# Second expert products half a round later, images unrolled, and the causal mask by a GpSimd select after the exponentials

## The chip, the cores and the metric

One core of a Trainium2 chip runs the whole program. The metric is device time in microseconds, the median of several executions. A profile records one execution of its own. The core has five engines that matter here: TensorE (PE, its weight loads PEld), VectorE (DVE), ScalarE (ACT), GpSimd (POOL) and SyncE (SP), which issues most DMAs. Each works through its own list of instructions in order, and they meet at semaphores.

## The reference

For 8 images of 1024 tokens with 96 channels: `x = x + moe_conv(groupnorm(x))`, then `t = t + attention(layernorm(t))`, then `t = t + moe_ffn(layernorm(t))`.

```python
# conv block, 8 experts, 2 of them gated in for each token (softmax over the two)
h = gelu(x @ W1[e] + b1[e]);  y = h @ W2[e] + b2[e];  out = sum_e gate[e] * y
# attention, 6 heads of 16 channels, causal over 1024 tokens
att = softmax(where(causal, q @ k.T / 4, -inf));  y = att @ v;  out = y @ w_proj.T + b_proj
# token block, 4 experts (hidden 384 in both blocks), the two largest probabilities, renormalised
```

Every expert is computed for every token; the gates of the others are zero.

## The kernel before

**Split precision.** An activation is kept as the sum of a high and a low half-precision part. A first-layer product of 128 hidden rows and 512 tokens (`first_layer`, out of `w1h`, `w1l` and `xah`, `xal` or `xch`, `xcl`) is three matmuls into one of two banks `ps_u`. ScalarE reads the bank twice with a gelu: to `hid` (32 bits, L933) and to `hidh` (16 bits, L934). GpSimd subtracts, `hidl = hid - hidh` (L628). The second layer (`second_layer`) takes for each tile of 128 tokens six products of 96 columns with `hidh` and then three with `hidl`, into `ps_y`. VectorE multiplies the four tiles of a group by the gates and adds them to `acc`, `x1` or `xo` (`combine`, L1104), and frees the bank.

**Rounds and slots.** A group is one expert on 512 tokens. An iteration has 16 groups of the conv block (phase 0) and 8 of the token block (phase 1), of different images. `rounds` yields for each round the group that goes up (first layer) and the one that goes down (second layer), which is the group before. A round has four slots, with `j` the slot within the round: first-layer product `j` at slots 0, 1 and 2; second-layer tiles none, 0, 1, and 2 with 3 at slots 0 to 3. The wait for all of a group's `hidl` (`hl_ready`) stands in front of the first `hidl` product of tile 0, so behind the first-layer product of slot 1. `hidh` and `hidl` have two buffers.

**Chores.** The rest of the images' work is placed into slots by hand (`schedule`): norms (`ln1`, `ln2`, `gn_...`), routing, the biases (`bias_a`, `bias_c`), `qk` and `val`, and the 72 row maxima of an image (`max`, banks `ps_r`, reduced by VectorE at L1156), one a slot from slot 8. `maxima` then turns them and SyncE writes them as two more rows of `qs`. `ks` and `qs` are loaded through `qk_dram` once the scores of the image before are done.

**Softmax stage.** After the experts come 24 steps of `SOFT_STEPS`, each three heads by 128 keys by up to 512 queries. TensorE's order is scores of step n, then values of step n - 2 (`soft_scores`, `soft_values`). Scores go to five banks in turn (three of `ps_r`, two of `ps_u`). ScalarE takes the exponential into one of three `probs` buffers (L965) and TensorE multiplies with `vaug` into `ps_y`. On the 16 steps at the diagonal a fourth to sixth product per step, `mask_k` by `identb`, adds a very negative number where the key lies after the query.

**Iterations.** `walk` has iterations 0, 1 and 2 written out, 3 to 6 as a loop on every engine (`Fori`; `Count` turns counters into expressions of the loop's register), and 7 to 10 written out. Iteration 0 has the conv block alone and splits the weights, 1 has no token block, 8 is attention alone with its maxima, 9 and 10 have the token block alone.

Of the kernel before, what the change touches and what calls it, by code (L numbers as in the profile page):

```python
# [48 lines left out]
FIRST_LOOP, END_LOOP = 3, NIMG - 1  # L49
# [4 lines left out]
class Count:  # L54


    def __init__(self, per):
        self.per, self.it, self.k = per, None, 0

    def enter(self, it):  # L60
        self.at_entry = self.k
        self.it, self.k = it, self.k - FIRST_LOOP * self.per

    def leave(self):
        n = self.k + FIRST_LOOP * self.per - self.at_entry
        assert n == self.per, (n, self.per)
        self.it, self.k = None, self.at_entry + (END_LOOP - FIRST_LOOP) * self.per

    def value(self, times=1, plus=0):
        k = self.k * times + plus  # L70
        return k if self.it is None else self.it * (self.per * times) + k
# [18 lines left out]
def walk(eng, counts, iteration):  # L90
# [3 lines left out]
    with eng.Fori(FIRST_LOOP, END_LOOP) as it:  # L94
        for c in counts:
            c.enter(it)
        iteration(it, True, True, True)
    for c in counts:
        c.leave()
    iteration(NIMG - 1, True, True, True)  # L100
# [92 lines left out]
def schedule(it):  # L193
# [42 lines left out]
    beside_c = [(1, "bias_c", 0), (4, "bias_c", 1), (5, "ln1", 0), (6, "ln1", 1), (10, "ln1_apply", 0),  # L236
# [36 lines left out]
def shared_uses():  # L273

    return sum(CHORES[name][1] for phase in schedule(None) for at in phase.values() for name, _, _ in at)


# [15 lines left out]
SOFT_STEPS = [(t, c, j) for t in range(2) for c in range(NC) for j in range(TC * (c + 1))]  # L293


def build(nc, x, cWg, cbg, cW1, cb1, cW2, cb2, w_attn, b_attn, w_proj, b_proj,
          fWg, fbg, fW1, fb1, fW2, fb2, out):
    nc.disable_value_cache = True
    with ExitStack() as ctx:
# [24 lines left out]
        mask_k = sb("mask_k", [P, P], BF16)  # L324
# [20 lines left out]
        hidh = sb("hidh", [P, 2, HT, CH], F16)  # L345
        hidl = sb("hidl", [P, 2, HT, CH], F16)
# [94 lines left out]
        s_full, p_ready = sem("s_full"), sem("p_ready")  # L441
        pv_step = sem("pv_step")
# [29 lines left out]
        def _(sp):  # L472
# [91 lines left out]
            walk(sp, [], iteration)  # L564

        @block.gpsimd
        def _(pool):
# [13 lines left out]
            for tile, value in ((identb, 0.0), (mask_q, 0.0), (mask_k, 0.0), (mpart, NEG), (mneg, 0.0)):  # L581
# [17 lines left out]
            g.affine_select(out=mask_k[:], in_=mask_k[:], compare_op=ALU.is_ge, fill=NEG, base=0,  # L599
                            pattern=[[1, P]], channel_multiplier=-1)  # L600
# [42 lines left out]
        def _(pe):  # L643
# [81 lines left out]
            def moes(it, moe_a, moe_c):  # L725
# [5 lines left out]
                for up, down, phase, slots in rounds(moe_a, moe_c):  # L731
# [25 lines left out]
                    if up:  # L757
                        grp.k += 1
# [600 lines left out]
```

## Time and profile before

| | us |
|---|---|
| median of 3 runs | 1535.99 |
| the runs | 1527.34, 1535.99, 1537.08 |
| profiled execution, first to last instruction (its span) | 1533.6 |
| TensorE busy in it | 1324.4 |
| ScalarE busy in it | 934.1 |
| VectorE busy in it | 893.8 |
| GpSimd busy in it | 716.0 |

The span is from an execution that was recorded by the profiler; the runs are executions that were only timed, so what lies around the span is told only by the distance of 1533.6 from those three times. Busy time of an engine doesn't count its waits. A matmul's recorded time has its way through the array in it, so two in a row overlap.

### The profile page before, as it was taken

How to read it: one execution, taken by the hardware profiler on the slowest of the kernel's cores; microseconds unless marked ns; L12 is line 12 of the kernel's file. 1: busy time of each engine (PE TensorE's matmuls, PEld its weight loads, DVE VectorE, ACT ScalarE, POOL GpSimd, SP SyncE). 2: the span in 40 equal slices, each digit the busy share in tenths (PEclk: the TensorE clock that was granted, in tenths of full speed). 3: DMA queues.
4: the chain of work that ended last, by engine and by line, in shares of the span. 5: the costliest groups of instructions: out<-in, count | busy, mean ns of one | idle time of the engine just before them, and what ended most of it. 6: DMA issues, size and time to landing. Idle time of an engine off the chain costs nothing.

```text
span 1533.6 us, 36404 instructions
## 1 busy us (share of the span) xinstructions
PE 1324.4 (86%) x12957; PEld 775.0 (51%) x12957; DVE 893.8 (58%) x2662; ACT 934.1 (61%) x1880; POOL 716.0 (47%) x656
## 2 busy tenths in 40 slices
PE   4778879888898899889898899888998898968978
PEld 1554543565536564466635565365644665333445
DVE  4865593388617784287724886177832866165362
ACT  2566537566675667656675667656676666703755
POOL 4765540467406572367605573075713665000355
PEclk9897998999999999899998999899999999956989
DMA  5000200300021000400004000210003000120100
GB/s 108 12 1 18 46 1 12 75 2 2 12 54 32 2 2 23 71 7 2 2 22 76 1 2 16 52 32 2 2 23 65 1 2 2 38 48 1 23 12 11
DMA packets 37424, 35.14 MB, mean 23 GB/s; under 512 B 26091, under 2 KB 28012, under 8 KB 37234
## 3 DMA queue, kind: packets, MB, share of 16 engines
q1 hardware_dynamic: 20594, 26.37, 8.8%
q10 hardware_dynamic: 16640, 6.29, 1.9%
q8 instruction: 113, 1.85, 0.5%
q14 instruction: 77, 0.63, 0.2%
HBM read 22.62 MB, written 9.63 MB: 21 GB/s over the span
## 4 chain that ended last, share of the span: by engine, by line
PE 30%; issue 26%; POOL 21%; DVE 13%; DMA 4%; ACT 2%; DVEq 1%; POOLq 1%; SPq 1%; ACTq 0%
POOL hidl L628 20%; PE ps_y L647 11%; PE ps_u L647 9%; PE ps_r L647 6%; DVE mpart L1156 4%; PE ps_m L647 3%; DVE xn L1138 1%; DMA ks<-qk_dram 1%; DMA qk_dram<-qk_l 1%; DVE acc L1104 1%; ACT hidh L934 1%; DVE yt L1288 1%; POOLq L608 1%; PE ps_m L666 1%; POOL rstd L609 1%
## 5 line engine op out<-in xcount | busy, mean ns | idle before, releaser
L628 POOL TENSOR_TENSOR hidl<-hid,hidh 128x512 f16<-128x512 f32 x576 | 670.7, 1185 | 686.2 <-ACT hidh L934 684.1
L933 ACT ACTIVATE hid<-ps_u 128x512 f32<-128x512 f32 x576 | 345.0, 599 | 391.8 <-PE ps_u L647 363.2
L1156 DVE TENSOR_REDUCE mpart<-ps_r 128x1 f32<-128x512 f32 (+2 forms) x576 | 297.3, 549 | 94.1 <-PE ps_r L647 79.8
L934 ACT ACTIVATE hidh<-ps_u 128x512 f16<-128x512 f32 x576 | 344.4, 598 | 0.0
L647 PEld LDWEIGHTS ps_y<-w2s,hidh 128*128 128x128 f16 x4608 | 276.4, 101 | 119.2 <-issue 24.1
L647 PE MATMUL ps_y<-w2s,hidh 128*128 128x96 f16 x4608 | 326.3, 210 | 8.0 <-DVE acc L1104 7.2
L647 PE MATMUL ps_r<-ks,qs 96*128 96x512 f16 (+2 forms) x576 | 199.9, 363 | 66.9 <-DVE mpart L1156 39.4
L647 PE MATMUL ps_y<-w2s,hidl 128*128 128x96 f16 x2304 | 231.0, 211 | 26.7 <-POOL hidl L628 26.6
L647 PE MATMUL ps_u<-xah,w1h 97*128 97x512 f16 x408 | 168.7, 414 | 29.8 <-ACT hidh L934 12.8
L965 ACT ACTIVATE probs<-ps_r 128x512 f32<-128x512 f32 (+3 forms) x352 | 152.9, 506 | 57.6 <-PE ps_r L647 57.2
L647 PE MATMUL ps_u<-xah,w1l 97*128 97x512 f16 x408 | 168.1, 412 | 0.0
L647 PE MATMUL ps_u<-xal,w1h 97*128 97x512 f16 x408 | 167.6, 411 | 0.0
L647 PEld LDWEIGHTS ps_y<-w2s,hidl 128*128 128x128 f16 x2304 | 145.0, 101 | 32.6 <-POOL hidl L628 31.7
L647 PE MATMUL ps_y<-probs,vaug 128*32 128x512 f32 (+3 forms) x1152 | 160.0, 499 | 0.1
L965 ACT ACTIVATE probs<-ps_u 128x512 f32<-128x512 f32 (+3 forms) x224 | 104.0, 517 | 27.9 <-PE ps_u L647 27.9
L1104 DVE SCALAR_TENSOR_TENSOR acc<-ps_y,gatesa,acc 128x96 f32<-128x96 f32 x448 | 109.6, 306 | 13.0 <-PE ps_y L647 11.4
L647 PEld LDWEIGHTS ps_r<-ks,qs 96*128 96x128 f16 x576 | 59.8, 104 | 111.0 <-DVE mpart L1156 68.3
L647 PE MATMUL ps_r<-qs,ks 98*128 98x512 f16 (+3 forms) x352 | 99.0, 334 | 9.1 <-DMA qs<-mtl 7.0
L647 PE MATMUL ps_r<-mask_q,identb 128*128 128x128 bf16 x384 | 90.8, 238 | 0.0
L1138 DVE TENSOR_SCALAR xn<-x,mv,rstd 128x96 f32<-128x96 f32 x128 | 83.2, 710 | 8.6 <-POOL rstd L609 8.1
L647 PEld LDWEIGHTS ps_u<-xah,w1h 97*128 97x128 f16 x408 | 42.2, 103 | 68.6 <-ACT hidh L934 27.0
L1047 DVE SCALAR_TENSOR_TENSOR qk_l<-ps_m,qk_h 96x512 f16<-96x512 f32 x32 | 22.0, 687 | 86.6 <-ACT qk_h L988 86.6
(188 smaller groups left out, 1582.0 us busy)
## 6 DMA issues: line engine op xcount, KB each, us to landing
rb<-rsum_dram SPq DMA_DIRECT2D x24, 256.0 KB, 4.2
qs<-qk_dram SPq DMA_DIRECT2D x24, 192.0 KB, 4.9
ks<-qk_dram SPq DMA_DIRECT2D x24, 192.0 KB, 4.8
xin<-in_x_dram ACTq DMA_DIRECT2D x8, 384.0 KB, 4.1
qk_dram<-qk_h SPq DMA_DIRECT2D x16, 192.0 KB, 3.1
qk_dram<-qk_l SPq DMA_DIRECT2D x16, 192.0 KB, 3.5
out_dram<-xo ACTq DMA_DIRECT2D x8, 384.0 KB, 3.0
w_raw<-in_L_conv_W_dram SPq DMA_DIRECT2D x8, 288.0 KB, 5.1
```

Of the source, the lines that this page charges most:

```text
L608: pool.drain()
L609: g.tensor_tensor(dst, dst, power[0:n, 0:dst.shape[1]], ALU.pow).then_inc(done, 1)
L628: g.tensor_tensor(hidl[:, grp.k % 2, j, :], hid[:, j, :], hidh[:, grp.k % 2, j, :], ALU.subtract).then_inc(hl_ready, 1)
L647: return nc.tensor.matmul(dst, lhsT, rhs, start=start, stop=stop, skip_group_check=True)
L666: last = nc.tensor.transpose(ps_m[0:D, P * i:P * (i + 1)], src[:, TC * c + i, :], ident[:])
L933: a.activation(hid[:, j, :], bank[:], ACT.Gelu, scale=1.0 / WS)
L934: a.activation(hidh[:, grp.k % 2, j, :], bank[:], ACT.Gelu, scale=1.0 / WS).then_inc(h_ready, 1)
L965: a.activation(probs[:, n % 3, g, 0:w], soft_bank(k)[:, 0:w], ACT.Exp, scale=float(HD) ** -0.5).then_inc(p_ready, 1)
L1047: return v.scalar_tensor_tensor(out=lo, in0=ps_m[0:D, :], scalar=scale, in1=hi, op0=ALU.mult, op1=ALU.subtract).then_inc(m_free, 1)
L1104: last = v.scalar_tensor_tensor(out=out[:, t, :], in0=ps_y[grp.k % 2][:, D * i:D * (i + 1)], scalar=r.gates[:, t, e:e + 1], in1=acc[:, t, ...
L1138: v.tensor_scalar(dst[:, t, :], src[:, t, :], mv[:, t, 0:1], rstd[:, t:t + 1], ALU.subtract, ALU.mult)
L1156: v.tensor_reduce(mpart[:, h, i, part:part + 1], ps_r[k % 3][:, 0:w], AX, ALU.max).then_inc(mx_free, 1)
```

## The change

It does five things. The loop of `walk` is gone: all iterations are written out. The buffers of `hidh` and `hidl` become three (`HB`), tiles 0 and 1 of the group going down are multiplied at slots 2 and 3, tiles 2 and 3 of it at slots 0 and 1 of the next round; VectorE's additions for a group move to slot 1 of that next round, and `bias_c` 1 from slot 4 to slot 6. In iterations with all three parts the scores of softmax step 0 are issued in the last round of the experts, ahead of the last group's second-layer products. The products with `mask_k` are gone, and so is the tile. In their place GpSimd sets the exponentials behind the diagonal to zero with one select per diagonal step, and the values of those steps wait for it (`causal`).

```diff
-FIRST_LOOP, END_LOOP = 3, NIMG - 1
+FIRST_LOOP = 3
+HB = 3
...
-    with eng.Fori(FIRST_LOOP, END_LOOP) as it:
...
+    for it in range(FIRST_LOOP, NIMG):
         iteration(it, True, True, True)
...
-    beside_c = [(1, "bias_c", 0), (4, "bias_c", 1), (5, "ln1", 0), (6, "ln1", 1), (10, "ln1_apply", 0),
+    beside_c = [(1, "bias_c", 0), (5, "ln1", 0), (6, "bias_c", 1), (6, "ln1", 1), (10, "ln1_apply", 0),
...
+DIAGONAL = [n for n, (t, c, j) in enumerate(SOFT_STEPS) if j >= TC * c]
...
+            def clear_future(n, b):
+                pool.wait_ge(p_ready, b.value(SU, (n + 1) * TR))
+                block = probs[:, n % 3, :, 0:P]
+                g.affine_select(out=block, in_=block, compare_op=ALU.is_ge, fill=0.0, base=0,
+                                pattern=[[0, TR], [1, P]], channel_multiplier=-1).then_inc(causal, 1)
...
                 for n in range(STEPS + 1):
+                    if attend and n in DIAGONAL:
+                        clear_future(n, Image(it, -1))
...
-                        if down and first:
...
-                        if down:
-                            for i in ((), (0,), (1,), (2, 3))[j]:
-                                second_layer(down, i)
+                        if older and j < 2:
+                            second_layer(older, grp.k - 2, 2 + j)
+                        if down and j >= 2:
+                            if j == 2 and early and not up:
+                                soft_scores(Image(it, -1), 0)
+                            if first:
...
+                            for i in (j - 2,) if up or j == 2 else (1, 2, 3):
+                                second_layer(down, grp.k - 1, i)
                         run_chores(m, chore, chores(it, phase, slot))
+                    older = down if up else None
...
-                    diagonal = P * j >= CH * c
-                    last = mm(soft_bank(k)[:, 0:w], ks[0:MROW + 2, h, P * j:P * (j + 1)],
-                              qs[0:MROW + 2, h, q0:q0 + w], True, not diagonal)
-                    if diagonal:
-                        last = mm(soft_bank(k)[:, 0:P], identb[:], mask_k[:], False, True)
-                    last.then_inc(s_full, 1)
+                    mm(soft_bank(k)[:, 0:w], ks[0:MROW + 2, h, P * j:P * (j + 1)],
+                       qs[0:MROW + 2, h, q0:q0 + w]).then_inc(s_full, 1)
...
-                pe.wait_ge(p_ready, b.value(SU, (n + 1) * TR))
+                if n in DIAGONAL:
+                    pe.wait_ge(causal, b.value(len(DIAGONAL), DIAGONAL.index(n) + 1))
+                else:
+                    pe.wait_ge(p_ready, b.value(SU, (n + 1) * TR))
...
+                early = moe_a and attend and moe_c
+                moes(it, moe_a, moe_c, early)
+                softmax(it, Image(it, -1), attend, early)
...
                             if j == 0:
-                                wait(act, y_full, grp.value(1, -1))
+                                wait(act, y_full, grp.value(1, 1 - HB))
...
+                        if older and slot % TC == 1:
+                            combined(it, older)
+                    if down and not up:
+                        combined(it, down)
+                    older = down if up else None
```

## Rows read from the trace of the kernel before

**Rows 1.** The page: busy time by engine, and the chain by line, whole span.
```profile
PE 1324.4 (86%) x12957; PEld 775.0 (51%) x12957; DVE 893.8 (58%) x2662; ACT 934.1 (61%) x1880; POOL 716.0 (47%) x656
...
POOL hidl L628 20%; PE ps_y L647 11%; PE ps_u L647 9%; PE ps_r L647 6%; DVE mpart L1156 4%; PE ps_m L647 3%; DVE xn L1138 1%; DMA ks<-qk_dram 1%; DMA qk_dram<-qk_l 1%; DVE acc L1104 1%; ACT hidh L934 1%; DVE yt L1288 1%; POOLq L608 1%; PE ps_m L666 1%; POOL rstd L609 1%
```

**Rows 2.** Busy time by engine, clock and DMA of stretches (A:B us, length first).
```profile
core 0: us, PE busy (x) PEld busy (x) DVE busy (x) ACT busy (x) POOL busy (x), PEclk, DMA share, GB/s
275.20:411.30 136.10, 118.59 (x1355) 80.61 (x1349) 97.90 (x290) 84.29 (x157) 87.54 (x78) 0.96 0.11 22
450.80:587.50 136.70, 119.99 (x1351) 79.88 (x1343) 95.70 (x280) 85.01 (x157) 87.49 (x78) 0.95 0.12 22
...
804.90:943.10 138.20, 122.01 (x1351) 81.45 (x1343) 95.85 (x280) 84.61 (x156) 87.82 (x78) 0.93 0.12 23
982.60:1123.00 140.40, 122.36 (x1352) 80.87 (x1347) 95.92 (x280) 84.79 (x158) 87.90 (x78) 0.93 0.12 22
1162.50:1299.60 137.10, 121.38 (x1322) 80.50 (x1315) 90.42 (x270) 83.25 (x155) 86.80 (x76) 0.93 0.11 19
765.30:804.90 39.60, 39.39 (x276) 14.64 (x276) 11.72 (x48) 31.98 (x79) 0.00 (x0) 1.00 0.07 21
804.90:812.70 7.80, 3.92 (x35) 2.07 (x27) 0.69 (x1) 1.28 (x1) 0.00 (x0) 0.72 0.69 134
```

**Rows 3.** Table of waits, whole span: who <- for whom: us, times, longest.
```profile
PEld ps_u L647 <- ACT hidh L934: 34.3, 63, 3.6
...
PE ps_r L647 <- DVE mpart L1156: 39.4, 33, 2.9
...
PE ps_y L647 <- POOL hidl L628: 26.6, 34, 2.4
```

**Rows 4.** Timeline of the last iteration: start us, us, engine, line, operation, tiles.
```profile
1507.30 0.99 DVE L1104 SCALAR_TENSOR_TENSOR acc<-ps_y,gatesc,acc 128x96 f32<-128x96 f32 x4 [2.80 <-PE ps_y L647]
...
1511.10 0.99 DVE L1104 SCALAR_TENSOR_TENSOR acc<-ps_y,gatesc,acc 128x96 f32<-128x96 f32 x4 [2.80 <-PE ps_y L647]
...
1512.91 3.39 POOL L628 TENSOR_TENSOR hidl<-hid,hidh 128x512 f16<-128x512 f32 x3 [0.41 <-ACT hidh L934]
```

**Rows 5.** Timeline at the turn from iteration 4 to 5.
```profile
809.78 0.61 PE L647 MATMUL ps_u<-xah,w1h 97*128 97x512 f16 x1 [3.88 <-issue]
...
811.41 1.28 ACT L933 ACT_TABLE_LOAD   x1 [6.53 <-PE ps_u L647]
```

**Rows 6.** Table of waits of TensorE, 1160 to 1180 us (iteration 7).
```profile
PE ps_r L647 <- DMA ks<-qk_dram: 3.5, 1, 3.5
```

**Rows 7.** Timeline, end of the experts and start of the softmax stage, iteration 5.
```profile
936.49 0.58 SPq L529 DMA_DIRECT2D qs<-mtl  x1
...
941.34 0.30 PE L647 MATMUL ps_y<-w2s,hidl 128*128 128x96 f16 x3 [0.88 <-POOL hidl L628]
...
942.62 0.38 PE L647 MATMUL ps_r<-qs,ks 98*128 98x512 f16 x1
...
942.84 0.22 PE L647 MATMUL ps_r<-mask_k,identb 128*128 128x128 bf16 x1
...
942.90 0.38 PE L647 MATMUL ps_r<-qs,ks 98*128 98x512 f16 x1
...
943.10 1.57 ACT L965 ACTIVATE probs<-ps_r 128x512 f32<-128x512 f32 x3 [1.90 <-PE ps_r L647]
...
945.62 1.06 PE L647 MATMUL ps_y<-probs,vaug 128*32 128x512 f32 x6
```

**Rows 8.** Timeline, last step of the softmax stage of iteration 5.
```profile
982.03 0.28 ACT L965 ACTIVATE probs<-ps_u 128x128 f32<-128x128 f32 x1 [1.35 <-PE ps_u L647]
...
982.16 1.50 PE L647 MATMUL ps_y<-probs,vaug 128*32 128x384 f32 x18
982.21 0.44 ACT L965 ACTIVATE probs<-ps_r 128x128 f32<-128x128 f32 x2
```

**Rows 9.** Groups of GpSimd by line and form: xcount | busy us, mean ns.
```profile
L589 POOL TENSOR_SCALAR_AFFINE_SELECT group<-group 96x96 f32<-96x96 f32 x1 | 0.6, 551 | 0.1
...
L597 POOL TENSOR_SCALAR_AFFINE_SELECT mask_q<-mask_q 128x128 bf16<-128x128 bf16 x1 | 0.3, 292 | 0.0
```

**Rows 10.** Chain of the work that ended last: start us, us, what.
```profile
231.11 2.02 DMA qs<-mtl
```

More of the change, by code:

```diff
@@ L54, with __init__ @@
 class Count:
[L57 to L67, printed above, removed]
+    def __init__(self):
+        self.k = 0
     def value(self, times=1, plus=0):
-        k = self.k * times + plus
-        return k if self.it is None else self.it * (self.per * times) + k
+        return self.k * times + plus
 class Image:
@@ L344, in build @@
         hid = sb("hid", [P, HT, CH])
-        hidh = sb("hidh", [P, 2, HT, CH], F16)
-        hidl = sb("hidl", [P, 2, HT, CH], F16)
+        hidh = sb("hidh", [P, HB, HT, CH], F16)
+        hidl = sb("hidl", [P, HB, HT, CH], F16)
         class Routing:
@@ L580, in _ @@
             pool.drain()
-            for tile, value in ((identb, 0.0), (mask_q, 0.0), (mask_k, 0.0), (mpart, NEG), (mneg, 0.0)):
+            for tile, value in ((identb, 0.0), (mask_q, 0.0), (mpart, NEG), (mneg, 0.0)):
                 g.memset(tile[:], value)
@@ L712, in second_layer, with moes @@
                 if i == 0:
-                    pe.wait_ge(h_ready, grp.value(HT, 0))
-                    wait(pe, y_free, grp.value(1, -2))
+                    pe.wait_ge(h_ready, HT * (n + 1))
+                    wait(pe, y_free, n - 1)
                 for j in range(HT):
                     for part in range(2):
-                        mm(out, hidh[:, n % 2, j, tok], w2s[:, e * HT + j, part, :], j == 0 and part == 0, False)
+                        mm(out, hidh[:, n % HB, j, tok], w2s[:, e * HT + j, part, :], j == 0 and part == 0, False)
                 if i == 0:
-                    pe.wait_ge(hl_ready, grp.value(HT, 0))
+                    pe.wait_ge(hl_ready, HT * (n + 1))
                 for j in range(HT):
-                    last = mm(out, hidl[:, n % 2, j, tok], w2s[:, e * HT + j, 0, :], False, j == HT - 1)
+                    last = mm(out, hidl[:, n % HB, j, tok], w2s[:, e * HT + j, 0, :], False, j == HT - 1)
                 if i == TC - 1:
                     last.then_inc(y_full, 1)
-            def moes(it, moe_a, moe_c):
+            def moes(it, moe_a, moe_c, early):
                 starts = isinstance(it, int) and it == 0
                 first = True
+                older = None
                 if moe_a:
@@ L833, in soft_values, with softmax @@
                 last.then_inc(pv_step, 1)
-            def softmax(it, b, attend):
+            def softmax(it, b, attend, early):
                 for n in range(STEPS + 2):
-                    if n < STEPS and attend:
+                    if n < STEPS and attend and not (early and n == 0):
                         soft_scores(b, n)
@@ L1024, in _ @@
         def _(dve):
-            m, grp = Count(shared_uses()), Count(GA + GC)
-            his = Count(sum(name in ("x1_turn", "x2_turn", "qk") for phase in schedule(None)
-                            for at in phase.values() for name, _, _ in at))
+            m, grp = Count(), Count()
+            his = Count()
             v = nc.vector
@@ L1108, in combine, with combined @@
                 grp.k += 1
+            def combined(it, group):
+                last = group.e == (EA, EC)[group.moe] - 1
+                if last and group.c == 0 and group.moe == 0:
+                    wait(dve, x1r_ready, Image(it, 0).value(1, 0))
+                if last and group.c == 0 and group.moe == 1:
+                    wait(dve, out_done, image_c(it).value(16, 0))
+                combine(group, (x1, xo)[group.moe] if last else acc)
             def moes(it, moe_a, moe_c):
+                older = None
                 for up, down, phase, slots in rounds(moe_a, moe_c):
```

55 lines of the change are left out of this document (18 added, 37 removed).

## The prediction

> **What bounds the kernel now.** I read the page's busy table first [rows 1]: TensorE is busy for 86% of the span, ScalarE 61%, VectorE 58%, GpSimd 47%. So TensorE is the engine to follow. A busy share can hide stalls and a lowered clock, though, and the chain of work that ended last passes GpSimd's `hidl` (20%) more often than any product of TensorE [rows 1]. I therefore cut the span into stages [rows 2]. An iteration of the steady part (numbers 2 to 7) is a stretch of 136 to 140 us from the last exponential of one softmax stage to the first of the next (16 experts' groups of the conv block, 8 groups of the token block, and everything beside them), and a softmax stage of about 39.6 us. In the softmax stage TensorE is busy for 39.39 of 39.60 us at full clock (1.00, that is the level of 2.4 GHz), ScalarE for 31.98 and GpSimd for none. In the expert stretch TensorE is busy for about 121 of 138 us and the clock stands at 0.93 to 0.96, so there it falls for short times to its lower level of 1.2 GHz. The two stages have different limits: the softmax stage is TensorE's own work, the expert stretch is TensorE's work plus stalls in which it waits in order.
>
> What those stalls are is told by the table of waits [rows 3]: TensorE waits for VectorE's row maxima (39.4 us), for `hidl` of GpSimd (26.6), and its weight loads for `hidh` of ScalarE (34.3; part of that is covered by the product before). The cleanest picture of a group is at the very end, where little but the groups runs [rows 4]: VectorE's additions of the four tiles, one set per group, start at 1507.30 and 1511.10, so a group takes 3.80 us, while GpSimd's three subtractions take 3.39.
>
> **The change, part by part.** Five parts; I sum against the span of 1533.6 us and add 2.4 us at the end, the distance from that span to the median of the three runs (1535.99). The lowest run, 1527.34, is shorter than the profiled span, so this distance is no constant of the chip.
>
> *Loop unrolled.* The back edge is visible: between iterations 4 and 5 TensorE issues nothing for 3.88 us, comes back with the slow product form (0.61 us where 0.38 is usual), and ScalarE loads its table only 6.53 us after its last exponential [rows 5]. Iterations 4, 5 and 6 begin so (4 to 6 are reached through the branch, 3 falls into the loop). In the first 7.8 us TensorE is busy for 3.9, at a mean clock of 0.72 [rows 2]. But the whole price isn't got back: the unrolled iteration 7 waits 3.5 us for `ks` to land [rows 6] (iteration 2 does the like), a wait that the slow start hides in the loop. So I compare whole stretches [rows 2]: 136.7, 138.2, 138.2 and 140.4 us inside the loop against 136.1 for iteration 2, a difference of 0.6 + 2.1 + 2.1 + 4.3 = 9.1 us, and against 137.1 for iteration 7 (which has less to do), 5.1 us. I take 7, bounds 0 to 12. More code would be a cost if straight code had to wait for its fetching; iterations 2 and 7 are straight code and are no slower than the loop's, so I cost that at nothing, and the bound of 0 stands for the case that it isn't. The Trainium skill, page "Runtime: NRT & Kernel Launch", section "Instruction fetch mechanics", says that a taken branch whose target lies outside the current pages stops execution until a fetch is done; the 3.88 us agree, and by that rule the gain would be three such gaps, 11.6 us.
>
> *Mask products removed.* Of 24 steps of a softmax stage 16 touch the diagonal; each has three products of 128 columns. On a step of width 512 the score product starts at 942.62, its mask product at 942.84, the next score product at 942.90 [rows 7]. So a mask costs 0.06 us of TensorE, and 16 x 3 x 0.06 = 2.9 us a stage, 23 us for eight. ScalarE is the next limit of the stage. It is busy for 31.98 us of the 39.60 [rows 2], TensorE would be at 36.7. But the three exponentials of width 512 take 1.57 us [rows 7], those of width 128 0.62 [rows 8], while TensorE's part falls less steeply with the width, so on the 12 steps of width 512 both are level and part of the saving turns into waiting. I take 17 us, bounds 12 to 23.
>
> *The select on GpSimd.* It lies idle in this stage [rows 2], so only latency counts: `soft_values` of a diagonal step now waits for exponentials, then the select. The nearest rows are the selects of 128x128 (292 ns) and of 96x96 in inner runs of three (551 ns) [rows 9]. By the first, 384 elements a partition cost 0.88 us, by the second 2.2; the new one has inner runs of 128, so I take 0.85, and 0.1 us for each semaphore. What covers it is the distance from the end of a step's exponentials to its values: 945.62 less 944.67 is 0.95 us at the first step [rows 7]; at the last, the exponentials end at 982.65 and the eighteen values of the last three steps, which start at 982.16, are over at 983.66 [rows 8], so the last six (0.4 us by that row's mean or less) start about 0.6 us behind them. In between the two steps' lead holds, and I expect 1 to 3 us. So it is hidden except at the end, where the last two values follow at once: some 0.3 us a stage, 2.5 us in all. If TensorE becomes faster the cover shrinks, as its two steps' lead is what makes it. Bounds 0 to 12. Nothing else is queued on GpSimd behind a select but the next select and the first `hidl` of the next iteration, which needs a product of that iteration anyway.
>
> The Trainium skill speaks against this part: "GPSIMD Engine Reference", section "Elementwise — side-by-side cycle accounting", gives about 12 cycles an element where a body branches on data. By that figure one select would be 3.84 us (an estimate from the page). The 128x128 select [rows 9] works out at 2.3 ns an element and doesn't bear it out.
>
> *Early scores of step 0.* Now the last group waits with TensorE empty: its first `hidl` products start at 941.34 after 0.88 us of waiting, and the scores come at 942.62, the first exponentials at 943.10, the first values at 945.62, held by the bank that the second step's exponentials free [rows 7]. With step 0's scores and the two older tiles put in front, the idle time has work, and the exponentials may start when ScalarE's table load is done, 941.2. TensorE then has the last four tiles to 942.3, the scores of steps 1 and 2 and a transpose (some 1.3 us), and VectorE's last additions are done about 943.4. The values can start at 943.8 to 944.2, 1.4 to 1.8 us sooner, 0.5 of which is already counted as masks. In six iterations 8 us, bounds 0 to 13. The new risk is the wait for the maxima's rows of `qs` standing in front of the last products: their second load is issued at 936.49 [rows 7], and such a load took 2.02 us where the chain of work passed it [rows 10]. TensorE would come to it near 939, so I cost it at nothing; a landing 1 us later would cost 6 us.
>
> *Later second products.* In each round tile 0 and 1 are now at slots 2 and 3, tiles 2 and 3 of the group before at slots 0 and 1. A third buffer of `hidh` and `hidl` pays for it. The wait for `hidl` comes a slot later, when GpSimd (1.13 us each) has long finished, and slots 0 and 1 have a tile's 0.38 us of work in front of the wait for ScalarE. TensorE's own need is 9 first-layer products of 512 columns, 0.22 us each (the distance from a score product to the next instruction), and 4 tiles of 0.38 us (from 941.34 to 942.62 go three tiles and the last third of the first) [rows 7], 3.5 us; GpSimd's three subtractions take 3.39 [rows 4]. So a bare group may go from 3.80 to about 3.5 us: 0.3 x 192 groups = 58 us would be the outermost. Most groups aren't bare: the conv groups have a row maximum in each slot that fills the same holes, and VectorE, busy for 96 to 98 us of the stretch [rows 2], gives the pace where its chores stand in front of a reduction. I therefore go by the waits that exist [rows 3]: four fifths of the 26.6 us on `hidl` (21) and a quarter of the 34.3 on `hidh` (9), minus 4 that return as waits for VectorE's maxima. 26 us, bounds 8 to 42. The third part of the change here, `bias_c` 1 moved to slot 6 and the additions moved to slot 1 of the next round but one, keeps VectorE's work the same; `ln1` 1 already stood at slot 6, so its statistics wait at most half a group, hidden by the four slots to `ln1_apply`.
>
> *Given back.* The load of `ks` starts from the last scores, not from the experts, and its landing is fixed; slots 0 to 7 get shorter. In iteration 7 it costs 3.5 us now [rows 6]; shorter groups before slot 8 add some 0.6 us seven times: 4 us.
>
> Sum: 1533.6 - 7 - 17 + 2.5 - 8 - 26 + 4 = 1482.1; with 2.4 around it, 1484.5 us, say 1484.
>
> **Rivals.** (a) *The experts' stretch is VectorE's and GpSimd's.* For it: 39.4 us of waits for maxima already, and GpSimd's 3.39 us a group. Then the second products give the lower bound of 8, and the time is 1502. Against it: neither is busy for more than 96 of 138 us. (b) *Everything at its far bound*, since fewer holes also keep the clock at its upper level: the clock is 0.93 to 0.96 in the stretch [rows 2]. Then 9 + 23 + 13 + 42 less 6.5 is 80 us: 1456. (c) *It doesn't do what it says*: the waits for `hidl` turn one for one into waits for maxima and for `ks`, and the softmax stage is ScalarE's. Left are 5 (loop) and 12 (masks), less the 6.5 of the tails and loads: 1525. (d) *The select becomes the bound of the softmax stage*, the one way to end slower. Without masks TensorE's steps are about 1.4 us on average (36.7 us less some 3 of chores, over 24), `probs` has three buffers, and the diagonal steps stand in runs of 4, 8 and 4. A select of s us costs 16 x (s - 1.4) a stage once s is above 1.4; against the 54 us gained elsewhere it decides from s = 1.8 us. At 2.2 us, the dearer row of [rows 9], it adds 102 us: 1586. By the figure of the Trainium skill named above it would be this rival, and worse. For it: the dearer row exists, and VectorE, whose work might slow GpSimd, is busy for 11.72 us of the stage [rows 2]. Against it: the dearer row has inner runs of three elements, the new one of 128.
>
> **How the numbers follow.** The forecast 0.58; (a) 0.18; (b) 0.13; (c) 0.07; (d) 0.04. A measurement of this kernel tells about 1% from no change (its own three runs spread by 0.6%). Slower than 1551 is (d) alone, 0.04; within 1% (above 1520.6) is (c) and a little of (a), 0.08; the rest is faster by over 1%, 0.88. The forecast alone would span 1468 to 1500; the range takes in (a), and most of (b): 1455 to 1512.
>
> **What would show it.** No idle 6.5 us on ScalarE at the turn of an iteration; `hidl` gone from TensorE's waits; a bare group in the last iteration of about 3.5 us; softmax stages of 36 to 37 us with GpSimd busy in them, selects of 0.7 to 1.0 us, and values that never name the select but at the end of a stage; the first values within 2.5 us of the first exponential being ready to run. A select of 1.5 us or more, or a bare group still at 3.8, would make the sum wrong at once. A stretch that stays at 136 us with all waits on VectorE's maxima would be rival (a).

## The result, and the profile after

The changed kernel takes 1519.14 us (median of 4 runs, 1512.0 to 1521.14) beside 1533.68 us of the kernel before (4 runs): ratio 0.9888, 95% interval 0.9858 to 0.9918. It is faster by about 17 us (1.1%) where 52 were forecast, and the time lies outside the range. The profiled execution is the one of 1521.14 us, span 1519.3. Times are medians of the timed executions, without one slow execution each of e8, e12, e13 and e17 (4198.95, 2345.87, 1521.72 and 1532.98 us).

The page of the changed kernel, busy time by engine (first line) and the chain by line (second), against [rows 1]:

```profile
PE 1309.2 (86%) x12573; PEld 757.5 (50%) x12573; DVE 904.2 (60%) x2662; ACT 946.4 (62%) x1880; POOL 785.3 (52%) x782
...
PE ps_y L636 20%; PE ps_u L636 18%; PE ps_r L636 9%; PE ps_m L636 6%; DVE mpart L1156 5%; DVE xn L1138 4%; DMA qk_dram<-qk_l 3%; DVE acc L1097 3%; DMA ks<-qk_dram 3%; POOL hidl L615 2%; DVE yt L1288 2%; PE ps_m L655 1%; ACT hidh L928 1%; DVEq L1140 1%; SPq L505 1%
```

`hidl` fell from 20% of the chain to 2%, and TensorE's own products took its place. Most of that fall isn't the later products' work. The chain of e1, which has only the loop written out, passes `hidl` for 4%. By engine the page of before has, first, and that of e1, second:

```profile
PE 30%; issue 26%; POOL 21%; DVE 13%; DMA 4%; ACT 2%; DVEq 1%; POOLq 1%; SPq 1%; ACTq 0%
```

```profile
PE 49%; DVE 24%; DMA 7%; POOL 5%; issue 5%; ACT 4%; DVEq 3%; SPq 2%; POOLq 1%; ACTq 0%
```

So the 20% that the prediction started from belonged to the trace of the loop. TensorE is busy for 15 us less, nearly what the kernel gained. Now the stages, the view of [rows 2]; the last row is the softmax stage:

```profile
core 0: us, PE busy (x) PEld busy (x) DVE busy (x) ACT busy (x) POOL busy (x), PEclk, DMA share, GB/s
271.50:407.30 135.80, 117.65 (x1332) 79.09 (x1327) 96.25 (x279) 86.43 (x157) 88.93 (x79) 0.95 0.12 23
445.20:585.30 140.10, 122.75 (x1330) 81.83 (x1325) 97.42 (x279) 86.43 (x156) 88.89 (x79) 0.91 0.12 22
800.40:938.40 138.00, 121.69 (x1331) 81.00 (x1326) 96.73 (x279) 86.51 (x157) 88.89 (x79) 0.93 0.11 22
976.30:1117.10 140.80, 123.71 (x1332) 82.87 (x1327) 96.65 (x279) 86.63 (x158) 89.15 (x79) 0.92 0.11 22
1155.00:1289.00 134.00, 117.64 (x1294) 78.02 (x1289) 90.61 (x266) 85.38 (x154) 87.79 (x77) 0.94 0.11 20
762.20:800.40 38.20, 37.40 (x247) 12.25 (x247) 11.88 (x48) 31.91 (x79) 7.82 (x15) 1.00 0.08 22
```

The softmax stage went from 39.6 to 38.2 us. The experts' stretch stayed where it was: 138.0 for 138.2, 140.8 for 140.4, and the six of iterations 2 to 7 together 828 for 827. The column PEclk is what to look at: 0.91 to 0.95 where it was 0.93 to 0.96 [rows 2]. TensorE's clock has two levels, 1.2 and 2.4 GHz, so a mean of c in a stretch of t us means 2(1 - c)t us at the lower one. Over the stretches of iterations 2 to 7 together the trace's clock record gives 102.4 us at the lower level before, 119.5 after.

The table of waits over the whole span, lines of TensorE, against [rows 3]:

```profile
PE ps_r L636 <- DVE mpart L1156: 51.5, 34, 3.1
PE ps_r L636 <- DMA ks<-qk_dram: 34.9, 8, 10.2
PE ps_u L636 <- ACT hidh L928: 17.5, 25, 3.1
PE ps_m L788 <- DVE mneg L1164: 11.1, 8, 3.3
...
PE ps_m L655 <- DVEq L1140: 8.1, 8, 2.0
...
PE ps_y L636 <- DVE acc L1097: 7.2, 3, 3.7
...
PE ps_y L636 <- POOL hidl L615: 3.9, 4, 1.5
```

The wait for `hidl` went from 26.6 us to 3.9, so here the change did what it says. The wait for row maxima went from 39.4 to 51.5; 10 of these 12 us come with the written-out loop alone (e1). And the timeline of the last iteration, against [rows 4]:

```profile
1506.71 0.99 DVE L1097 SCALAR_TENSOR_TENSOR acc<-ps_y,gatesc,acc 128x96 f32<-128x96 f32 x4 [2.44 <-PE ps_y L636]
1510.19 0.99 DVE L1097 SCALAR_TENSOR_TENSOR acc<-ps_y,gatesc,acc 128x96 f32<-128x96 f32 x4 [2.49 <-PE ps_y L636]
```

A bare group takes 3.48 us, 3.80 before: the forecast's 3.5. The select, in the page's groups:

```profile
L587 POOL TENSOR_SCALAR_AFFINE_SELECT probs<-probs 128x384 f32<-128x384 f32 x128 | 66.7, 523 | 306.5 <-ACT probs L959 306.4
```

So three local signs of the forecast were there (`hidl` nearly gone from TensorE's waits, bare group 3.5, select cheap), the softmax stage is 38 us for the 36 to 37 of the forecast's signs, and 35 us of the gain weren't there. The question of the experiments is where they went.

### The profile page after: what moved, and what is told of

Same layout as the page of the kernel before. It is cut to its first block, busy times and chain, and to the rows that moved or that the text cites. A ratio compares the mean times of both kernels' runs of the same rounds, so it can differ in the third digit from the quotient of the medians.

```text
span 1519.3 us, 32843 instructions
## 1 busy us (share of the span) xinstructions
PE 1309.2 (86%) x12573; PEld 757.5 (50%) x12573; DVE 904.2 (60%) x2662; ACT 946.4 (62%) x1880; POOL 785.3 (52%) x782
## 4 chain that ended last, share of the span: by engine, by line
PE 55%; DVE 23%; DMA 7%; issue 4%; DVEq 3%; ACT 3%; POOL 3%; SPq 2%; POOLq 0%; ACTq 0%
PE ps_y L636 20%; PE ps_u L636 18%; PE ps_r L636 9%; PE ps_m L636 6%; DVE mpart L1156 5%; DVE xn L1138 4%; DMA qk_dram<-qk_l 3%; DVE acc L1097 3%; DMA ks<-qk_dram 3%; POOL hidl L615 2%; DVE yt L1288 2%; PE ps_m L655 1%; ACT hidh L928 1%; DVEq L1140 1%; SPq L505 1%
## 5 line engine op out<-in xcount | busy, mean ns | idle before, releaser
L636 PEld LDWEIGHTS ps_y<-w2s,hidh 128*128 128x128 f16 x4608 | 289.7, 101 | 166.3 <-issue 38.5
L636 PE MATMUL ps_y<-w2s,hidh 128*128 128x96 f16 x4608 | 336.5, 212 | 7.2 <-DVE acc L1097 7.2
L636 PE MATMUL ps_r<-ks,qs 96*128 96x512 f16 (+2 forms) x576 | 203.6, 369 | 88.6 <-DVE mpart L1156 51.5
L587 POOL TENSOR_SCALAR_AFFINE_SELECT probs<-probs 128x384 f32<-128x384 f32 x128 | 66.7, 523 | 306.5 <-ACT probs L959 306.4
L959 ACT ACTIVATE probs<-ps_u 128x512 f32<-128x512 f32 (+3 forms) x224 | 104.0, 518 | 21.3 <-PE ps_u L636 12.8
L636 PE MATMUL ps_r<-qs,ks 98*128 98x512 f16 (+3 forms) x352 | 92.1, 334 | 7.3 <-DMA qs<-mtl 7.3
L636 PEld LDWEIGHTS ps_u<-xal,w1h 97*128 97x128 f16 x408 | 42.2, 103 | 58.0 <-issue 15.9
```

Source lines behind the costliest of these rows:

```text
L587: g.affine_select(out=block, in_=block, compare_op=ALU.is_ge, fill=0.0, base=0, pattern=[[0, TR], [1, P]], channel_multiplier=-1).then_inc ...
L636: return nc.tensor.matmul(dst, lhsT, rhs, start=start, stop=stop, skip_group_check=True)
L959: a.activation(probs[:, n % 3, g, 0:w], soft_bank(k)[:, 0:w], ACT.Exp, scale=float(HD) ** -0.5).then_inc(p_ready, 1)
```

## The experiments

Each run is compared with the kernel before on its own chip, so two runs are compared by their ratios, given behind each time with their 95% intervals. "Stretches" is the summed length of the six experts' stretches of iterations 2 to 7, "low" the time in them at 1.2 GHz, both in us, of the profiled run (before 827 and 102.4, after 828 and 119.5). The profiled executions of the main runs, in us ("not busy" is the span less TensorE's busy time):

| | span | TensorE busy | not busy | low |
|---|---|---|---|---|
| before | 1533.6 | 1324.4 | 209.2 | 102.4 |
| e1, loop written out | 1524.8 | 1310.2 | 214.6 | 75.1 |
| after | 1519.3 | 1309.2 | 210.1 | 119.5 |
| e2, masks back | 1531.7 | 1322.5 | 209.2 | 105.8 |
| e3, no early scores | 1527.5 | 1303.2 | 224.3 | 109.2 |
| e4, old order | 1499.5 | 1291.4 | 208.1 | 78.5 |
| e14, additions only | 1509.9 | 1295.5 | 214.4 | 78.5 |
| e17, additions at slot 3 | 1508.1 | 1284.7 | 223.4 | 88.7 |

### One part at a time

*e1*, only the loop written out in the kernel before:
```
-    with eng.Fori(FIRST_LOOP, END_LOOP) as it:
+    for it in range(FIRST_LOOP, NIMG):
```


> The kernel before with the loop written out and nothing else changed. Theory A (the load of ks is a fixed latency behind the last scores, about 14 us from the last score to the first row maximum, and the loop's slow start hid inside it): no gain, 1531 to 1537 us, the loop's 3.9 us gap on TensorE replaced by 3 to 5 us of waiting for ks in each of iterations 3 to 6. Theory B (as predicted): 7 us faster, about 1527.

1526.55 us, 0.9943 (0.9916 to 0.9970): 8.8 us gained. Two rows of waits before:

```profile
PE ps_r L647 <- DMA ks<-qk_dram: 25.4, 6, 10.4
...
PE ps_u L647 <- issue: 11.8, 3, 4.1
```

and three of e1, with the maxima's to be read beside [rows 3]:

```profile
PE ps_r L642 <- DVE mpart L1151: 49.4, 37, 3.2
PE ps_r L642 <- DMA ks<-qk_dram: 36.5, 8, 10.2
PE ps_y L642 <- POOL hidl L623: 27.7, 37, 2.4
```

The gap at the turn, 11.8 us on "issue", is gone, and the wait for `ks` has grown by 11.1, as theory A said. TensorE's time not busy even rose, from 209.2 to 214.6. What fell is its busy time, by 14.2 us for the same products, and low fell by 27.3, half of which is 13.7. The timed executions say the same: at a mean granted clock of 0.930 and 0.931 the kernel before took 1527.91 and 1529.94 us, and e1 at 0.931 took 1527.48 and 1528.13.

*e2*, the change with the mask products back and without the select:
```
-    if attend and n in DIAGONAL: clear_future(n, Image(it, -1))
+    if diagonal:
+        last = mm(soft_bank(k)[:, 0:P], identb[:], mask_k[:], False, True)
```


> The changed kernel with the mask products back and no select. Theory A: softmax stages 1.7 to 2.2 us longer each, and since the stage's end sets the start of the ks load nothing of it is hidden: 14 to 18 us slower than the changed kernel, about 1535. Theory B: 17 us slower, the same. Rival: the select costs what the masks saved, then no difference, 1519.

1534.19 us, 0.9984 (0.9957 to 1.0011): the masks' removal is worth 0.0096 of the time, 14.7 us, known to some 6 us by the two intervals. The softmax stages are 39.8 us here and 37.9 with the select. In the profiled executions the eight stages together are 18.2 us shorter with the select, and the six stretches 6.3 us longer, with 13.7 us more at the lower clock.

*e3*, the change with `early = False`.


> The changed kernel with the scores of step 0 back behind the last second-layer products. Theory A: the whole softmax stage starts 1.3 to 1.8 us later in six iterations and the ks load with it: 8 to 10 us slower, about 1528. Rival: the early scores are worth nothing because ScalarE's table load at 941 sets the start anyway: 1519 to 1522.

1530.16 us, 0.9968 (0.9937 to 1.0): the early scores are worth 11 to 12 us, known to some 7. They took 14.2 us out of TensorE's time not busy, and 6.0 came back as busy time, with 10 us more at the lower clock.

*e4*, the change with the second products, VectorE's additions and `bias_c` 1 in their old slots:
```
-    if older and j < 2: second_layer(older, grp.k - 2, 2 + j)
...
-    for i in (j - 2,) if up or j == 2 else (1, 2, 3):
+    for i in ((), (0,), (1,), (2, 3))[j]:
         second_layer(down, grp.k - 1, i)
...
-    if older and slot % TC == 1: combined(it, older)
+    if down: combined(it, down)
```


> The changed kernel with the second-layer tiles and VectorE's additions in the old slots (tiles 0, 1, then 2 and 3 at slots 1, 2, 3), all else kept. Theory A (beside a row maximum in each slot TensorE had no holes to fill, the gain is 0.3 us for each group without one only): about 15 to 20 such groups, 5 to 8 us slower, 1525. Theory B (as predicted): 26 us slower, 1545. Theory C (the later products delay chores of VectorE and cost in the conv groups what they gain at the ends): same time, 1515 to 1521.

1498.98 us, 0.9753 (0.9695 to 0.9810). Without the later second products the kernel is 20 us *faster* than the change, where all three expectations had it level or slower. This is the part that lost what the others won. Stretches 805, low 78.5. The window of iteration 5 of e4 (from last to first exponential, as above):

```profile
795.20:929.40 134.20, 118.14 (x1321) 79.37 (x1316) 96.52 (x279) 84.34 (x157) 88.04 (x79) 0.95 0.12 23
```

Iteration 5 is 3.8 us shorter (134.2 for 138.0), of which 3.55 is TensorE's *busy* time (118.14 for 121.69); 20.5 us of it ran at the lower clock after, 13.7 in e4. Over the whole span it is 17.8 of 19.8 us. TensorE's waits in that stretch add up to 15.8 us after and 15.7 in e4. These rows differ by more than 0.3 us, first after:

```profile
PE ps_u L636 <- ACT hidh L928: 1.4, 3, 0.9
PE ps_m L788 <- DVE mneg L1164: 1.0, 1, 1.0
PE ps_m L655 <- DVEq L1140: 0.9, 1, 0.9
```

and e4:

```profile
PE ps_y L636 <- POOL hidl L615: 2.5, 5, 0.9
...
PE ps_u L636 <- ACT hidh L926: 0.5, 2, 0.4
```

The 2.5 us on `hidl` are gone, and 0.9 on `hidh`, 1.0 on `mneg` (the row maxima, negated, on their way to `qs`) and 0.9 on VectorE's queue at the normalised x (`xn`) have come. The timeline of TensorE in that stretch shows one such exchange. In e4:

```profile
903.96 0.30 PE L636 MATMUL ps_y<-w2s,hidl 128*128 128x96 f16 x3 [0.55 <-POOL hidl L615]
...
905.95 0.28 PE L636 MATMUL ps_r<-ks,qs 96*128 96x256 f16 x1 [1.68 <-DVE mpart L1152]
```

and after:

```profile
914.01 0.28 PE L636 MATMUL ps_r<-ks,qs 96*128 96x256 f16 x1 [2.43 <-DVE mpart L1156]
```

What TensorE no longer waits for `hidl` it waits at the next row maximum, 2.43 us for 0.55 and 1.68. So what the part saves in waits comes back in other waits, and what it loses on top is clock.

*e15 and e16*, the change and e4 again on one chip, 11 runs of before beside them.


> The changed kernel itself, for the comparison on one chip: ratio 0.989 to the kernel before, as it was.

> The old order (e4) itself on the same chip: ratio 0.975 to the kernel before, 18 to 22 us below the changed kernel. Rival: the two chips differed, and it is less than 10 us below it.

1519.43 us (0.9895, 0.9860 to 0.9931) and 1496.63 (0.9748, 0.9690 to 0.9807): 22.8 us apart (the intervals leave some 10 us either way). The clock goes along with the time within one kernel too: the eight executions of e15 run from 1507.46 us at a mean granted clock of 0.923 to 1522.47 at 0.910, and e16's four have 0.929 to 0.936.

*e8*, the later order in iterations 0, 9 and 10 alone, where the groups are bare.


> Later second products only in iterations 0, 9 and 10, where the rounds have no row maxima, and the old order in 1 to 8. A bare group went from 3.8 to 3.5 us in the profile of the changed kernel, and about 20 of the 32 groups of these iterations are bare: 3 to 6 us less than e4, about 1494. Rival: what these groups gain is given back in waits for the routing (as in iteration 9): 1498 to 1500.

1498.72 us, 0.9788 (0.9763 to 0.9814), no better than e4. Of TensorE's waits over the span, the one for `hidl` is 4.2 us shorter than in e4 (21.3 for 25.5), and those for `yt`, `xal` at the turn and `wql` are 2.2, 2.0 and 1.6 longer: what the bare groups gain is given back there.

### Which half of the part

*e14*, e4 with only VectorE's additions (and `bias_c` 1) at their changed place.


> The old order of the tiles on TensorE with VectorE's additions where the change puts them (slot 1 of the next round; bias_c 1 at slot 6). If VectorE's half of the edit is what costs, this is as slow as the changed kernel, 15 to 20 us above the old order on the same chip. If it is TensorE's half, it is within 5 us of the old order. If both, about half way.

1514.26 us, 0.9882 (0.9824 to 0.9941), 17.6 us over e16 on the same chip. The profiled executions, 1509.9 and 1499.5 us (e4), show part of it: 6.3 us of time not busy, 4.1 of busy time, at the same low (78.5). The wait for `mneg` is 12.0 us over the span (4.9 in e4), as in the change (11.1). The timed executions differ in clock as well, 0.925 to 0.932 beside 0.929 to 0.936. So this half costs by waits and, in part, by clock.

*e13*, the change with the additions of one round of the token block at slot 27 for 25, behind two row maxima and the maxima's turn.


> The changed kernel, but in the one round with the turn of the row maxima (slots 24 to 27 of the token block) VectorE's additions come at slot 27, behind that chore, in place of slot 25. In the changed kernel TensorE waits 1.2 us for the maxima's last reduction in six iterations, in the old order 0.2. If the additions in front of it are the cause, 1 us in each of six iterations, 6 us less than the changed kernel on the same chip. Rival: the wait only moves to the end of the experts' stretch, no difference.

1503.89 us, 0.9845 (0.9765 to 0.9926): its interval overlaps e15's, so a gain is likely and not shown. The wait for `mneg` did fall by 6.2 us, from 11.1 to 4.9, as expected.

*e17*, the change with all additions at slot 3 of the next round, behind its chores, and with `bias_c` 1 and `ln1` 1 at slot 8 for 6. The tiles stay late, and the additions stand even later:
```
-    beside_c = [..., (6, "bias_c", 1), (6, "ln1", 1), ...
+    beside_c = [..., (8, "bias_c", 1), (8, "ln1", 1), ...
...
-    if older and slot % TC == 1: combined(it, older)
+    if older and slot % TC == 3: combined(it, older)
```


> The changed kernel with VectorE's additions of a round moved from slot 1 to slot 3 of the next one, behind that round's chores (the row maximum and what hangs on it). Theory that the additions' place is most of the loss: 1488 to 1500 us, ratio to the kernel before 0.970 to 0.978, last row maximum to first score back from 7.2 us to about 5.6. Rival, that TensorE's own late order of halves is the loss: 1510 to 1522 us, as the changed kernel, whose waits at the turns stay at 1 to 3 us each.

1524.37 us, 0.9941 (0.9915 to 0.9967): my theory that the additions' place was most of the loss fell. The profiled execution is the shortest of e17's, 1509.93 us at a granted clock of 0.923; the other eight took 1519.26 to 1531.84 at 0.906 to 0.916, so its low of 88.7 isn't typical. Its table of waits, whole span:

```profile
PE ps_y L636 <- DVE acc L1097: 47.3, 29, 5.0
PE ps_r L636 <- DVE mpart L1156: 43.7, 19, 3.9
...
PE ps_m L788 <- DVE mneg L1164: 4.9, 2, 3.3
```

The waits for maxima and for `mneg` shrink as hoped (51.5 to 43.7, 11.1 to 4.9), but now TensorE waits 47.3 us (7.2 after) until the additions have freed `ps_y`, which has two banks; its time not busy is 223.4 us for 210.1. Early additions hold up VectorE's chores, late ones hold up TensorE's products; with the tiles late, neither of the two places tried for all additions is free.

### The clock

*e6 and e7*: idle products of TensorE in front of its largest waits, at six places of the steady iterations (the text on record counts five). They multiply constants into columns of a `ps_y` bank that no tile uses, so the output is untouched:
```
+    def fill(n, b, back=1):
+        if b.value(1, 0) < NIMG - 1:
+            for _ in range(n):
+                mm(ps_y[(grp.k - back) % 2][:, TC * D:CH], identb[:], mask_q[:])
```
50, 40, 48 and 42 of them before row maximum 0, 23, 39 and 60, 30 before the second turn of x, 16 before the first of x2; in the change (e6) and in e4 (e7).


> The changed kernel with idle products (128 columns of identb and mask_q into unused columns of ps_y) in front of five places where TensorE waits 1.1 to 5 us in iterations 2 to 7: 50 before row maximum 0, 40 before 23, 48 before 39, 42 before 60, 30 before the second x_turn, 16 before the first x2_turn. At full clock they take 0.9 to 2.7 us each place and fit into the waits. Clock theory: the changed kernel is slower than e4 because its waits stand so that TensorE's clock falls to the lower level more often (119.6 us of the six expert stretches at the lower level against 78.6); with the waits filled both go away and it comes to 1480 to 1495. Rival: the low clock is only a trace of the waits and costs nothing by itself, or the later products cost by delaying work: 1517 to 1530, slower by what fillers don't fit.

> The same fillers in the old order (e4). Clock theory: with fillers in both the order hardly matters, so this is within 8 us of the filled later order, at 1480 to 1492. Rival, the later order costs by itself: this stays 15 to 20 us below the filled later order.

1484.83 us, 0.9685 (0.9665 to 0.9704) and 1482.98, 0.9667 (0.9645 to 0.9689). Low is 6.8 us in both. At equal clock the two orders are within 2 us of each other (4.6 in the profiled executions, 1486.6 and 1482.0). By the ratios the idle products gave the change some 31 us and e4 some 13.

*e11*, only 16 before the first x2 turn and 40 before maximum 23, in the change.


> The changed kernel with fillers at the neighbouring pair of waits alone (16 before the first x2_turn, 40 before row maximum 23), where it had 6.8 us at the lower clock in most iterations and the old order 3.4. Clock theory: this pair goes to full clock and gives 2 to 4 us in each of six iterations, 1500 to 1510. If the other waits cost as much, most of the 31 us of the five fillers stays out.

1508.62 us, 0.9833 (0.9787 to 0.9880): 8 us, a quarter of e6's gain, if it is one, as the interval overlaps the change's; low 78.5.

*e12*, the idle products in e1.


> The kernel before, unrolled (e1), with the five fillers and nothing else. The clock stood at 0.937 to 0.975 in its expert stretches (65 us at the lower level in six of them, against 119.6 in the changed kernel). Clock theory: it gains about 12 us against e1, less than half of the 31 us that the changed kernel gained: 1510 to 1516. Rival, fillers help by the timing of the waits and not by the clock: a gain of 25 to 30 us here too, 1500 or less.

1507.80 us, 0.9827 (0.9778 to 0.9877), low 0. The text counts 65 us at the lower clock in e1; the trace shows 75.1, half of it 37.5 us. The gain was 18 us, between the clock theory's 12 and the rival's 25 to 30. Half the low time is more than was won: some of the idle products' time comes on top of the waits, or the waits only move. This run doesn't tell the two apart.

### The fixed latencies

*e5*: e4, with the writes of q and k to `qk_dram` issued before SyncE's wait for the last scores, and all six loads behind it.
```
                 if s == 0:
-                    wait(sp, s_full, b.value(SU, 0))
-                wait(sp, qk_out, b.value(64, 32 * (s + 1)))
...
+                    return
+                wait(sp, s_full, b.value(SU, 0))
+                wait(sp, qk_out, b.value(64, 64))
...
```


> The kernel with the second-layer tiles in the old order (e4), and SyncE's writes of q and k to DRAM both issued before it waits for the last scores, so that behind them only the six loads remain. Theory: ks is late by a fixed latency behind the last scores; the profile of e4 has 3.1 to 4.7 us of waiting for it at slot 8 in iterations 2 to 6. Then this takes 2 to 4 us from each of seven iterations: 1499 to about 1480. Rival: the loads are limited by the DMA engines, six at once take as long as three after three, and the time stays at 1496 to 1500.

1484.69 us, 0.9667 (0.9626 to 0.9707), 13 us under e4 by the ratios, though the two intervals just touch. TensorE's wait for `ks` is 21.9 us over the span (36.8 in e4). SyncE at the turn into iteration 5, e4 and then e5:

```profile
794.63 1.27 SPq L505 DMA_DIRECT2D qs<-qk_dram  x3
795.94 0.42 SPq L499 DMA_DIRECT2D qk_dram<-qk_h  x1
796.41 0.43 SPq L499 DMA_DIRECT2D qk_dram<-qk_l  x1
801.60 1.26 SPq L505 DMA_DIRECT2D ks<-qk_dram  x3
```

```profile
795.36 1.26 SPq L506 DMA_DIRECT2D qs<-qk_dram  x3
796.66 1.37 SPq L506 DMA_DIRECT2D ks<-qk_dram  x3
```

In e4 the loads of `ks` are issued 7 us behind those of `qs`, as the writes of k stand between them and have to land first; in e5 1.3 us.

*e9, e10 and e18*: both together, with 20 idle products for 50 at maximum 0, in the change (e9), in e4 (e10) and in e17 (e18).


> The changed kernel with the fillers (20 in front of row maximum 0 in place of 50) and with the writes of q and k ahead of the wait for the last scores. If the clock and the ks load are two separate costs, both gains add: 1485 less about 13, 1468 to 1476. If the filled kernel has its ks wait hidden elsewhere, 1480 to 1485.

> The same two edits on the old order of the second-layer products. Clock theory: within 8 us of the later order with the same edits, 1466 to 1474. Rival, the later order costs by itself: 15 to 20 us less than it.

> The same with idle products at the five waits of iterations 2 to 7 and the early q and k writes. Additions' place: 1460 to 1470 us, beside 1464.7 of the old order with the same two additions. TensorE's late order: 1482 to 1492, as the 1490.0 of the late order with them.

| | us | ratio | span | TensorE busy | not busy | low |
|---|---|---|---|---|---|---|
| e6, for comparison | 1484.83 | 0.9685 | 1486.6 | 1332.3 | 154.3 | 6.8 |
| e7, for comparison | 1482.98 | 0.9667 | 1482.0 | 1332.1 | 149.9 | 6.8 |
| e9 | 1489.97 | 0.9708 (0.9670 to 0.9745) | 1486.6 | 1329.2 | 157.4 | 20.5 |
| **e10** | **1464.71** | 0.9552 (0.9497 to 0.9607) | 1463.9 | 1314.9 | 149.0 | 0 |
| e18 | 1525.26 | 0.9921 (0.9891 to 0.9950) | 1525.5 | 1344.8 | 180.7 | 75.1 |

e10 is the best version found, 69 us faster than before and 51 than the change by the ratios. In the old order the two gains add (18 us from e7 to e10); in the late order they don't. e9 missed both its expectations and isn't faster than e6, and e10 came out 25 us under e9, as its rival had it ("the later order costs by itself"), not within 8 us as the clock theory had it. e18 missed both of its own. Iteration 5's window of e10:

```profile
777.10:906.30 129.20, 122.66 (x1518) 86.84 (x1512) 96.12 (x279) 84.33 (x157) 88.72 (x79) 1.00 0.13 21
```

TensorE is busy for 122.7 of 129.2 us at full clock. 197 of its products are the idle ones (1518 for e4's 1321), some 12 us by the 0.06 us between a mask product and the next in [rows 7], an estimate. Its longest waits left there are 1.4 us for maxima and 0.9 for `hidl`. In e9's stretch of iteration 5 the normalised values `yt` come late instead:

```profile
PE ps_m L637 <- DVE yt L1301: 2.1, 1, 2.1
```

## Why the prediction was right or wrong

*Loop unrolled*, forecast -7 (0 to 12): the size was right, -8.8 by e1 (4.6 to 12.9 by its interval), the mechanism was not, so the size is partly luck. ScalarE's idle 6.5 us at the turn is gone, and no row of waits of TensorE's products names "issue" any more, so the straight code showed no wait for its fetching. But TensorE's time not busy didn't fall (209.2 to 214.6 us); the gain is 14.2 us of busy time, that is clock, which this term didn't have. The 11.6 us that the Trainium skill's branch rule would give (page "Runtime: NRT & Kernel Launch", section "Instruction fetch mechanics") lie in the interval. The trace agrees with the gaps (11.8 us in three), but not that they are the gain: the wait for `ks` rose from 25.4 us over the span to 36.5 in e1. The term *given back*, +4, named the right place and was too small by 7; the rise belongs to the loop and wasn't raised further by the other parts (34.9 after).

*Mask products*, -17, and *the select*, +2.5: together -14.5, and -14.7 measured by e2. The select took 0.52 us for my 0.85, and the waits for it (8.4 us over the span) are all on weight loads before `ps_y`; e2 takes the two terms together and doesn't tell them apart. Two slips of mine did no harm: by its row six of the eighteen last values take 0.5 us, not 0.4, and rival (b) has 9 for the loop where its bound was 12. Rival (d) is out. So is the Trainium skill's 12 cycles an element ("GPSIMD Engine Reference", section "Elementwise — side-by-side cycle accounting"), which would be 3.84 us a select: 523 ns for 384 elements is 1.4 ns an element. The stages are 37.9 us and not the 36 to 37 given as a sign, which contradicted my own sum: 14.5 us over eight stages are 1.8 a stage, 37.8. The early scores have no part in it, as the stages of e3, without them, are 37.8 too.

*Early scores*, -8 (0 to 13): -11 to -12 by e3, within the bounds, and by the mechanism named (14.2 us of TensorE's time not busy went). The wait for `qs` that I feared didn't come.

*Later second products*, -26 (8 to 42): **the step that failed.** Measured +20 to +23 (e4 against the change; e15 against e16). In the term's own words, "four fifths of the 26.6 us on `hidl` (21) and a quarter of the 34.3 on `hidh` (9), minus 4 that return as waits for VectorE's maxima":
- The first figure was right: 22.7 of the 26.6 us vanished.
- The 9 on `hidh` were not: the weight loads' row is 34.8 us after for 34.3 before, and TensorE's own wait for it is 17.5 us after, 11.9 in e4.
- The 4 that return, "as waits for VectorE's maxima", were far too few. From e4 to the change the waits fell by 21.6 on `hidl`, and rose by 2.6 on maxima, 6.2 on `mneg`, 7.7 on the normalisation's queue, 5.6 on `hidh` and 2.7 on `yt`: 24.8 in all. Behind a wait for `hidl` stood the next thing that was nearly as late, mostly out of VectorE's chain. This is near rival (c), "the waits for `hidl` turn one for one into waits for maxima and for `ks`", which I had at 0.07; one for one is right, but only 2.6 of the 24.8 went to maxima and none to `ks` (34.9 for 36.8).
- The stretches didn't get shorter (828 us for 827), which was the sign of rival (a), but of TensorE's 15.8 us of waits in iteration 5 only 7.8 are on VectorE's maxima.
- The clock had no term at all, except for the better in rival (b), with "fewer holes also keep the clock at its upper level". It went the other way: 119.5 us low for e4's 78.5. Half of 41 is 20.5 us, and TensorE's busy time rose by 17.8 us for the same products, where its time not busy rose by 2.0; the stretches are 828 against 805 us. With low at 6.8 in both, e6 and e7 are level (1484.8 and 1483.0), so the clock is enough to explain the loss between these two kernels.

The clock isn't the whole account of the late order, though. e14, with the additions alone moved, loses 6.3 us in time not busy at e4's low time, and e9 stays 25 us behind e10: in their profiled executions 14.3 us of busy time and 8.4 of time not busy.

What stays open: why the late order spends more time at the lower level when the sums of its waits are those of e4. Of e9's 14.3 us of busy time over e10, 10 are low time (20.5 us, halved); the rest, and the 8.4 of waits such as `yt`, the runs don't take apart. Nor do they show why e5's edit gains nothing in the late order. e18, where the additions are late, has 75.1 us low in spite of its idle products; its span is 38.9 us over e9's, 15.6 of it busy time and 23.3 not busy.

The sum of the parts holds as far as their intervals tell: 8.8 + 14.7 + 12 = 35.5 us for e4's 37.9, less 20 to 23 for the last gives 13 to 15, and 17 were measured.

## What to carry to other kernels

A wait that vanishes is a gain only if nothing else on that engine was nearly as late: before adding up a releaser's total, look at which stretches its waits stand in, and what the waiting engine needs next. Where an engine's work is reordered and the other engines follow in order, every buffer's releaser moves with it (here the additions were either ahead of VectorE's chores or too late for `ps_y`), so both ends of each buffer need a row of their own. And read a stretch by busy time and clock before its waits: 18 us of this kernel's loss, and all of the written-out loop's gain, showed in how long TensorE was busy with the same products, and idle products at six places won back 13 to 31.

## What of the hardware was not expected

- TensorE at 86% busy, with scattered waits of 1 to 3 us, spent 75 to 120 us of six stretches (about 820 us) at 1.2 GHz. Products that compute nothing, put in front of the largest waits, brought this to 0 to 7 us in e6, e7, e10 and e12, but left 20.5 in e9 and 75.1 in e18.
- A kernel change that hardly alters TensorE's time not busy (208.1 to 210.1 us) can move that time by 41 us (e4 to the change), and between executions of one kernel the clock moves the time by 15 us (e15).
- A chain of the work that ended last that is read from a loop can put the blame wrongly: `hidl` had 20% of it with the loop, 4% with the same code written out (e1).
- GpSimd's select of 128x384 values in runs of 128, in place, takes 523 ns, less per element than the 128x128 one of [rows 9] (292 ns).
